# A gather table with 128 rows for "nothing here" in place of one

## The reference

```python
edge_index = jnp.stack([src, dst])
x = _layernorm(x + _L0_gnn_ref(x, edge_attr_16, src, dst, ...))      # attention over the edges into each node
x = _layernorm(x + _L1_gnn_ref(x, edge_index, edge_weight, ...))     # attention, MLP on every node
x = _layernorm(x + _L2_gnn_ref(x, edge_index, L2_gnn_W, L2_gnn_b))
x = _layernorm(x + _L3_gnn_ref(x, src, dst, edge_weight, 100000))

# the end of _L0_gnn_ref:
msgs = x_t[src] * alpha[:, None]
h = jax.ops.segment_sum(msgs, dst, num_segments=N)
return h + bias
```

## Time and profile before

| | |
|---|---|
| median of 3 runs | 2801.25 us (2794.16 to 2805.04) |
| profiled execution, span from the first to the last instruction | 2797.4 us |
| PE busy | 1944.0 us (69%) |
| DVE busy | 1685.3 us (60%) |
| POOL busy | 1661.4 us (59%) |
| ACT busy | 1497.3 us (54%) |
| moved by DMA | 214.75 MB, mean 77 GB/s |

### The profile page before, as it was taken

How to read it: one execution, slowest core, us unless ns; L and a number is a source line. 1 busy time by engine, 2 the same in 40 slices (tenths; PEclk the granted TensorE clock), 3 DMA queues, 4 the chain that set the end, 5 groups by cost and what they waited for, 6 DMA issues and landing times. The chain is left out here.

```text
span 2797.4 us, 27574 instructions
## 1 busy us (share of the span) xinstructions
PE 1944.0 (69%) x8422; PEld 1002.8 (36%) x8422; DVE 1685.3 (60%) x3220; ACT 1497.3 (54%) x2242; POOL 1661.4 (59%) x1610
## 2 busy tenths in 40 slices
PE   6998778679988688888999868658888875000000
PEld 3444334227643233364444327543333434000000
DVE  4876699993888578745655433997656687000002
ACT  4777667553677568746787762337777652000000
POOL 6777777600037565000777757775777768677774
PEclk9999899886999789979999996559989885555555
DMA  3233222101668674102454491442111233100002
GB/s 63 66 68 81 58 56 68 51 30 45 203 126 58 47 56 52 46 16 71 139 144 137 118 228 53 120 121 67 52 52 53 89 105 98 55 17 22 22 21 96
DMA packets 235785, 214.75 MB, mean 77 GB/s; under 512 B 156783, under 2 KB 169926, under 8 KB 235638
## 3 DMA queue, kind: packets, MB, share of 16 engines
q1 hardware_dynamic: 181190, 166.34, 20.7%
q0 software_dynamic: 51200, 46.31, 12.2%
q10 hardware_dynamic: 3248, 0.34, 0.1%
HBM read 140.36 MB, written 86.04 MB: 81 GB/s over the span
## 5 line engine op out<-in xcount | busy, mean ns | idle before, releaser
L2372 POOL DMA_INDIRECT stab<-wk,rank_i x200 | 208.5, 1042 | 289.1 <-DVE wk L588 231.4
L545 ACT ACTIVATE b_s<-ps,vec 128x512 f32<-128x512 f32 (+1 forms) x356 | 240.9, 684 | 159.4 <-PE ps L624 59.8
L2369 POOL DMA_INDIRECT u<-x2tab,dpos_i x200 | 220.8, 1104 | 82.7 <-issue 77.8
L2369 POOL DMA_INDIRECT u<-x3tab,src_i x200 | 206.1, 1030 | 85.3 <-issue 59.2
L2369 POOL DMA_INDIRECT u<-in_x_dram,src_i x200 | 201.4, 1007 | 76.7 <-issue 59.8
L2369 POOL DMA_INDIRECT e_b<-x0tab,dpos_i x72 | 72.7, 1009 | 290.9 <-DVEq L2174 265.5
L2372 POOL DMA_INDIRECT out_dram<-u,dst_i x176 | 198.2, 1126 | 74.7 <-issue 59.8
L2369 POOL DMA_INDIRECT u<-in_x_dram,dst_i x200 | 201.1, 1006 | 64.4 <-issue 59.5
L2372 POOL DMA_INDIRECT out_dram<-u,sfin_i x200 | 196.5, 982 | 66.3 <-issue 66.3
L776 DVE TENSOR_SCALAR b_x<-b_s 128x8 f32<-128x8 f32 x2 | 0.3, 168 | 389.3 <-DMA b_gl<-out_dram 389.3
L533 PE MATMUL ps<-b_h,blk_c 128*128 128x512 f32 (+1 forms) x296 | 174.4, 673 | 57.9 <-ACT b_gl L553 57.4
(11 more groups left out here) (428 smaller groups left out, 5026.4 us busy)
## 6 DMA issues: line engine op xcount, KB each, us to landing
b_gl<-in_x_dram SPq DMA_DIRECT2D x98, 256.0 KB, 2.7
wk<-dlist SPq DMA_DIRECT2D x50, 500.0 KB
wk<-slist SPq DMA_DIRECT2D x50, 500.0 KB
out_dram<-b_gl SPq DMA_DIRECT2D x93, 256.0 KB, 2.0
u<-stab SPq DMA_DIRECT2D x25, 510.0 KB
x2none<-b_gl SPq DMA_DIRECT2D x25, 250.0 KB
wk<-x2none SPq DMA_DIRECT2D x25, 240.0 KB
x2tab<-wk SPq DMA_DIRECT2D x25, 240.0 KB
```

The lines of the kernel that those rows point to most:

```text
L545: return nc.scalar.activation(b_s[l][:, 0:w], pB[l][:, 0:w], ACT.Abs_reciprocal_sqrt, bias=col(EPSV))
L2369: pool.indirect_dma_start(out=o, out_offset=None, in_=tab, in_offset=at_ix(ix), **kw).then_inc(s, 16)
L2372: pool.indirect_dma_start(out=tab, out_offset=at_ix(ix), in_=a, in_offset=None, bounds_check=rows_n - 1, oob_is_err=False).then_inc(s, 16)
```

## The change

The table gets 128 rows for "no aggregate" in place of one, all with the bias. The index of a source without an aggregate was E; now it is E + p, where p is the partition at which that source stands in the index tile `la` (128 partitions x 512) when its place is worked out. `X["io"][:, 0:1]` holds 128 p. The sort has put neighbouring node numbers on the same partition; the edges of a gather have sources in random order.

```diff
+    NONES = 128
-    x0tab, x2tab, x2none, x3tab = (dram(n, (r, D)) for n, r in (("x0tab", E + 1), ("x2tab", E), ...))
+    x0tab, x2tab, x2none, x3tab = (dram(n, (r, D)) for n, r in (("x0tab", E + NONES), ("x2tab", E), ...))
...
-        B0, G1, ..., HB1, FUN = range(17)
+        B0, G1, ..., HB1, FUN, NONE = range(18)
...
             addr = X["la"]
             yield from address(addr, q, t, t2, 512)
             yield tick(1.2)
-            stt(addr, addr, -float(E), valid, ALU.add, ALU.mult)
-            ts(addr, addr, float(E), None, ALU.add)
+            ts(col(NONE), X["io"][:, 0:1], 1.0 / 128, float(E), ALU.mult, ALU.add)
+            stt(addr, addr, col(NONE), valid, ALU.subtract, ALU.mult)
+            ts(addr, addr, col(NONE), None, ALU.add)
...
             sp.wait_ge(S("w_made"), 1)
-            sp.dma_start(x0tab[E:E + 1, :], rowc[0:1, R_B0, :]).then_inc(S("x0_none"), 16)
+            sp.dma_start(x0tab[E:E + NONES, :], rowc[:, R_B0, :]).then_inc(S("x0_none"), 16)
```

More of the change, by code:

```diff
@@ L49, in gnn_resnorm_kernel @@
         dram(n, (FLAT,)) for n in ("q_spos", "q_ddeg", "q_dps", "q_sdeg", "q_dpos", "q_rank"))
-    x0tab, x2tab, x2none, x3tab = (dram(n, (r, D)) for n, r in (("x0tab", E + 1), ("x2tab", E), ("x2none", E), ("x3tab", E)))
+    x0tab, x2tab, x2none, x3tab = (dram(n, (r, D)) for n, r in (("x0tab", E + NONES), ("x2tab", E), ("x2none", E), ("x3tab", E)))
     stab = dram("stab", (E, RW))
@@ L140, in gnn_resnorm_kernel @@
         vec = sb("vec", [128, 20])
-        B0, G1, LB1, G2, LB2, MB2, MB1, L2B, FUS, EPSV, EPS2, CB0, CR, CT, C2, HB1, FUN = range(17)
+        B0, G1, LB1, G2, LB2, MB2, MB1, L2B, FUS, EPSV, EPS2, CB0, CR, CT, C2, HB1, FUN, NONE = range(18)
         rowc = sb("rowc", [128, 4, D])
```

## The result

The changed kernel's median is 2777.97 us (2774.48 to 2786.30, 4 runs); the kernel before has 2802.03 us (2794.16 to 2805.04, 4 runs). The ratio is 0.9919 with a 95% interval of 0.9892 to 0.9946: 22.7 us faster, between 15 and 30. A second set of 6 runs, beside other kernels, gave 2777.55 us and a ratio of 0.9904 (0.9874 to 0.9934). I had forecast 2768 us in a range of 2752 to 2790: the mechanism was right, its size was about 10 us too large.

What follows compares the result with a forecast made beforehand. Repeated reads of one row were taken to slow POOL's gather packets, delaying stores that ACT, PE and DVE wait for; 28.5 + 5.1 - 0.3 = 33.3 us off the 2801.25 us median gave 2768 us, range 2752 to 2790.

Steps and rivals of the forecast that it cites:

- Packets at 459 ns because one row is asked for again and again: POOL's layer-0 aggregate gathers, from 811 us: one repeated address makes packets cost 459 ns; spread rows should bring under 100 ns.
- ACT's store waits pay, and go: ACT's gelu, 811 to 1160 us: 28.5 us of waits for stores lie on the path; under 5 us should remain.
- The 200 gathers in 265 to 275 us: POOL's gathers of `x0tab[dpos]`: with the holds gone, all 200 are issued in 265 to 275 us, where they took 298.
- The sum, 28.5 + 5.1 - 0.3 = 33.3 us: Whole gain: ACT's store waits plus DVE's gather waits less the new DVE instruction, 33.3 us, uncut as POOL's limit is 33.
- The last add was forecast near 1090: DVE's adds of the gathered groups: the last of 25, at 1124.0 us before, should come near 1090.
- ACT's term: Part of the gain from ACT's waits for stores: 15.7 us (three longest waits) to 28.5 (all); 28.5 was taken.
- Without a DMA wait the adds came every 10.1 us: DVE's adds, 1053.08 to 1124.01 us: spacing of 10.1 us, used against the rival that the stage is bound by compute.
- the rival that compute takes the place: Sources' pipeline on DVE and PE can't run faster, waits only change names: gain 0 to 14 us; chance 0.12.
- Everything behind the stage keeps its length: After layer 1's first scatter: all later work keeps its length, so what the stage saves arrives at the end.
- The forecast 1293 for the first scatter: Layer 1's first scatter, on POOL: should move from 1326 to about 1293 us.
- What the clock of PE gave back: PE's slower matmuls after stalls: 0 to some 7 us, taken as 0 in the sum and left to the range.
- My 0.77: PE's granted clock from 900 to 960 us in the kernel before, cited for matmuls slowed after stalls.

Runs made afterwards that it cites:

- e1: Changed kernel with all its parts, but every index without an aggregate points at row E again; 2797.06 us, ratio 0.9976 to the kernel before.
- e2: Changed kernel with two rows for no aggregate, E for partitions 0 to 63 and E + 1 for 64 to 127; 2780.18 us, ratio 0.9907.
- e5: Kernel before, still one address, with the eleven marker stores (constant rows) placed 520 us later; 2791.59 us, ratio 0.9966.
- e6: Kernel before, still one address, with five own buffers for the sources' scaled rows and the marker stores 520 us later; 2789.92 us, ratio 0.9954.
- e4: Changed kernel with five own buffers for the sources' scaled rows, so the gelu no longer waits for their store; 2775.10 us, ratio 0.9892.
- e8: Changed kernel again without an edit, 6 runs beside other kernels; 2777.55 us, ratio 0.9904 to the kernel before.
- e3: Kernel before, still one address, with five own buffers for the sources' scaled rows, so the gelu no longer waits for their store; 2817.47 us, ratio 1.0044.

## Why the prediction was right, and what was too large

1. *Packets at 459 ns because one row is asked for again and again*: right. 77 ns after (forecast under 100), 10.3% of the engines (11 to 14); e1 and e2 show that it is the address and not the region or another part of the change. The landing fell to 2.5 us (about 3).
2. *ACT's store waits pay, and go*: right, 2.4 us left (forecast under 5). e5 and e6 lower these waits without touching the address, and PE's idle time in the stage follows. The 2.4 us lie between the none that I took and the 4.7 us that I had estimated by the rule of the Trainium skill's "DMA: Bandwidth & Descriptors", section "Queues, rings and completion order", by which an engine takes turns between its queues by packets. No run here shows the turns themselves.
3. *The 200 gathers in 265 to 275 us*: 269.1. One hold of POOL above 3 us is left, 6.37 us before 1031 us. It ends 0.8 us after the end of the add at 1029.90, which came 19.4 us after the add before it; between the two ACT waits for no DMA.
4. *The sum, 28.5 + 5.1 - 0.3 = 33.3 us, "no reason to cut it"*: this is the step that was mis-sized. It measured 21.8 us in the stage. The last add was forecast near 1090, which is 278 us after the first gather; it came after 288. I had followed only the longest waits through three engines and then counted all of ACT's and DVE's. The row to count from was the earlier trace rows: PE's wait for this gelu fell by 21.0 us, though its 35.0 us alone don't tell how much of it would go. PE's whole idle time in the stage fell by 22.2. The rest of ACT's and DVE's waiting had lain beside PE's own work, as e4 confirms: with none of these waits left, its stage is 492.2 us. My lower bound for ACT's term, 15.7, and the upper, 28.5, held; the value should have come between them.
5. *"Without a DMA wait the adds came every 10.1 us"*: that was taken from seven adds in the end of the stage, and it wasn't quite without such waits: ACT waited 0.87 us for a store at 1054.44 and 0.31 at 1111.63. Over all 25 the changed kernel has (1104.12 - 828.54) / 24 = 11.5 us, where POOL unheld would bring a group each 10.6. So the rival that compute takes the place was not the outcome, but a third of the forecast gain (11.5 of 33.3 us) did not come, with PE busy 422 of 493 us.
6. *Everything behind the stage keeps its length*: right as far as one can tell. From the first scatter of layer 1 to the first output scatter it is 874.7 us, and 879.3 in e8 (before: 2200.7 - 1326.4 = 874.3). The forecast 1293 for the first scatter became 1309.0, of which 4.4 us came before the stage began. Those 4.4 are not shown to be the change's: e6, which lacks the change, begins at 817.6 us. But all seven profiled executions with spread addresses begin at 815.4 us or later, and the other four with one address at 810.9 to 814.6; the cause stays open.

What the clock of PE gave back I had left out, at 0 to 7 us. Over the stage it gave back nothing: PE is busy 422.0 us before and 422.5 after, at the same mean clock, 0.87. My 0.77 was that of one window of 60 us, and a later one goes the other way: from 1020 to 1080 us the kernel before has 0.91 and the changed one 0.86.

## What to carry to other kernels

An index that stands for "nothing" is a row that most of a gather may ask for; two or more copies of it, picked by anything that varies within the gather, take the load off one address (here 459 ns a packet became 107 with two rows). The sign to look for is a queue that is busy far beyond its bytes. The price is paid by whoever shares the engines, here mostly by stores, so a deeper buffer for one store may only hand the wait to the next (e3). To size such a gain, look for the busiest engine of the stage (here PE) and count its idle time that ends on the late work, not the waits of the engine that is late itself.

## What the runs showed that I had not expected

- Two neighbouring rows are enough, and even a single eighth of the reads moved to the next 256 bytes brings the whole gain within the noise (2780.88 us), though packets still take 266 ns.
- Beside gathers of one address the issue of a store on SP, 0.25 to 0.6 us otherwise, took up to 21.4 us, and a store landed as late as 40.2 us after it (e3).
- The same changed kernel, profiled twice, had spans 14.4 us apart with stages only 0.5 us apart.
